# The copy of the first Q group of each query tile, moved from VectorE to ScalarE

## The reference

```python
q, k, v = (einsum('bsm,hmd->bhsd', x, kernel[i]) for i in (0, 1, 2))
attn = softmax(einsum('bhsd,bhtd->bhst', q, k) / (64*64*16))
x = layernorm(x + einsum('bsf,fm->bsm', (attn @ v)_as_b_s_f, WO[0]))
x_prev = x shifted by one token
r = sigmoid((mu_r*x + (1-mu_r)*x_prev) @ W_r.T)
kk = (mu_k*x + (1-mu_k)*x_prev) @ W_k.T
x = layernorm(x + r * (square(relu(kk)) @ W_v.T))
```

## Time and profile before

| | |
|---|---|
| median of 3 runs | 2562.26 us (2561.67 to 2564.42) |
| profiled execution | 2560.9 us, span 2559.4 us on the slowest core |
| spans of the 8 cores | 2553.3 to 2559.4 us |
| PE busy | 2079.9 us, 81% |
| ACT busy | 1245.6 us, 49% |
| DVE busy | 833.8 us, 33% |
| granted TensorE clock, mean of the slowest core | 0.893 |

### The profile page before, as it was taken

The page is one execution under the profiler, slowest core; times in us unless marked ns, Lnnn a source line. Parts: engine busy times, 40 slices in busy tenths (PEclk is TensorE's granted clock), DMA queues, the critical chain, the costliest instruction groups (busy, mean ns, idle before and its releaser), DMA issues.

```text
span 2559.4 us, 29992 instructions; the slowest of 8 cores (2553.3 to 2559.4 us)
## 1 busy us (share of the span) xinstructions
PE 2079.9 (81%) x10062; PEld 709.3 (28%) x10176; DVE 833.8 (33%) x1369; ACT 1245.6 (49%) x1441; POOL 20.2 (1%) x27
## 2 busy tenths in 40 slices
PE   0998888798888978896898888878978897889835
PEld 0442222232222222232342222222222232223212
DVE  0330014233341525053550140432434052504356
ACT  0017855756375637653006556475627663665520
POOL 0000000000000000000000000000000000000000
PEclk9998888898989989898899999988888898889867
DMA  9359600013100420033221130101310041002201
GB/s 182 46 81 203 164 12 23 1 67 97 52 1 34 116 66 1 34 99 83 33 50 33 40 109 34 34 1 66 83 66 1 34 116 66 1 1 72 99 28 65
DMA packets 83056, 153.04 MB, mean 60 GB/s; under 512 B 1952, under 2 KB 16352, under 8 KB 82912
## 3 DMA queue, kind: packets, MB, share of 16 engines
q1 hardware_dynamic: 51184, 102.87, 12.4%
q0 software_dynamic: 23024, 31.47, 8.6%
q10 hardware_dynamic: 8704, 16.78, 1.9%
HBM read 151.12 MB, written 31.46 MB: 71 GB/s over the span
## 4 chain that ended last, share of the span: by engine, by line
PE 58%; ACT 20%; DVE 11%; issue 8%; another core or an unknown queue 2%; ACTq 1%; DMA 1%; DVEq 0%; POOLq 0%
PE psg L99 29%; ACT pb L109 13%; PE pspv L99 11%; PE psden L99 11%; ACT lta L109 5%; PE psa L99 4%; PE psb L99 3%; DVE xka L118 2%; DVE rg L118 2%; DVE stv L118 2%; ACT rcr L109 1%; DVE recb L118 1%; DVE y L118 1%; DVE xra L118 1%
## 5 line engine op out<-in xcount | busy, mean ns | idle before, releaser
L109 ACT ACTIVATE pb<-psa 128x1024 bf16<-128x1024 f32 x512 | 522.8, 1021 | 381.7 <-PE psa L99 380.4
L109 ACT ACTIVATE pb<-psb 128x1024 bf16<-128x1024 f32 x512 | 523.8, 1023 | 363.8 <-PE psden L99 191.4
L99 PE MATMUL pspv<-pb,vtb 128*64 128x512 bf16 x2048 | 429.4, 427 | 19.9 <-DVE aba L118 19.8
L99 PE MATMUL psden<-pb,cstb 128*32 128x512 bf16 x2048 | 412.6, 411 | 0.0
L99 PE MATMUL psg<-xra,ws 128*128 128x512 bf16 x1264 | 342.1, 421 | 9.3 <-issue 8.9
L99 PE MATMUL psa<-qtb,ktb 64*128 64x512 bf16 x1024 | 214.6, 406 | 142.9 <-ACT pb L109 82.9
L118 DVE TENSOR_TENSOR aba<-pspv,rsb 128x512 bf16<-128x512 f32 x64 | 44.3, 692 | 766.7 <-ACT rsb L109 765.7
L99 PE MATMUL psb<-qtb,ktb 64*128 64x512 bf16 x1024 | 208.4, 401 | 62.2 <-ACT pb L109 62.2
L99 PEld LDWEIGHTS pspv<-pb,vtb 128*64 128x64 bf16 x2048 | 111.0, 109 | 282.6 <-issue 282.6
L99 PEld LDWEIGHTS psg<-xra,ws 128*128 128x128 bf16 x1320 | 128.1, 105 | 198.9 <-issue 93.3
L99 PE MATMUL psg<-aba,ws 128*128 128x512 bf16 x373 | 96.5, 413 | 87.4 <-DMA aba<-xT 78.1
(11 more groups left out here) (113 smaller groups left out, 1680.6 us busy)
## 6 DMA issues: line engine op xcount, KB each, us to landing
ws<-wsc SPq DMA_DIRECT2D x34, 2048.0 KB, 9.6
ws<-wts POOLq DMA_DIRECT2D x8, 2048.0 KB, 22.4
y<-xT SPq DMA_DIRECT2D x8, 2048.0 KB, 13.1
outT<-outb ACTq DMA_DIRECT2D x32, 512.0 KB, 4.6
wsc<-ws SPq DMA_DIRECT2D x7, 2048.0 KB, 16.1
xra<-xT POOLq DMA_DIRECT2D x6, 1024.0 KB, 12.7
aba<-xT POOLq DMA_DIRECT2D x4, 1024.0 KB, 13.4
rg<-xT POOLq DMA_DIRECT2D x4, 1024.0 KB, 9.7
```

What stands on the lines that cost most here:

```text
L99: i = e.matmul(_o, _l, _r, start=_st, stop=_sp, tile_position=_tp, skip_group_check=True)
L109: i = e.activation(_o, _i, _f, scale=_s, bias=_b)
```

## The change

The copy of Q group 0 of each tile is made by ACT (`AF.Copy`) instead of DVE. Its bank is freed by `c_ar` instead of `c_vg`, and the scores of head pair 0 wait for `c_ar`. Since the counter now differs, `qev` holds the counter beside the value. Groups 1 to 7 stay as they were. Eight copies of an execution are moved, one for each query tile.

```diff
                 def qevac(b):
-                    wait("v", c_g)
-                    nv = vop("tensor_copy",
-                             (QTB[:, oc * QT:(oc + 1) * QT], b.ap[:, :]),
-                             inc=c_vg)
-                    b.free = (c_vg, nv)
-                qev[oc] = 0
+                    if oc == 0:
+                        wait("a", c_g)
+                        nv = act(QTB[:, 0:QT], b.ap[:, :], AF.Copy, inc=c_ar)
+                        b.free = (c_ar, nv)
+                        qev[oc] = (c_ar, nv)
+                    else:
+                        wait("v", c_g)
+                        nv = vop("tensor_copy",
+                                 (QTB[:, oc * QT:(oc + 1) * QT], b.ap[:, :]),
+                                 inc=c_vg)
+                        b.free = (c_vg, nv)
+                        qev[oc] = (c_vg, nv)
                 proj_group(WS[2], oc, xbch, qevac)
-                qev[oc] = c_vg.n
...
                     if kt == 0 and qev.get(hp):
-                        wait("t", c_vg, qev[hp])
+                        wait("t", qev[hp][0], qev[hp][1])
```

## The result

The changed kernel takes 2522.85 us (median of 9 runs); the kernel before has 2564.85 us over its 10 runs by now. The ratio is 0.9843, with a 95% interval of 0.9820 to 0.9867: about 40 us or 1.6% faster. The profiled execution took 2517.97 us, against 2560.9 us before: 42.9 us less. Some executions of every kernel are slower on one die, at a lower granted clock; ratios and comparisons leave them out.

What follows compares the result with a forecast made beforehand. PE was taken to pace the kernel, idling for DVE's late copy. Six tiles gain 43.8 us, first tiles lose 0.9: 42.9 off 2560.9 gives 2518.0, median 2519 us, range 2505 to 2531.

Steps and rivals of the forecast that it cites:

- What the wait is, and that it goes: First scores, six non-first tiles: PE idles 9.57 us for a copy behind DVE's chain; on ACT, scores start 8.73 us earlier.
- That DVE is the next to be late, at the fourth Q group: Fourth Q group needs the second's bank, freed by DVE behind its chain: PE waits 1.87 us.
- One of the signs of being wrong that I named: At a tile's start: the idle that precedes the previous tile's adds grows; no size given.
- The cap of 9.0 us: Start of the fourth Q group: DVE's bank limits the gain to 397.20 - 388.20 = 9.0 us a tile.
- That the wait brings the low clock, one group's worth a tile: After the new wait, one Q group at the lower clock in each of six tiles, costing 1.69 us each.
- The likeliest case: One Q group at low clock after the new wait in each of six tiles: 2519 us, chance 0.50.
- the clock stays up: Rival: no clock drop after the new wait before the fourth Q group; gain 53.1 us, 2509 us, chance 0.22.
- Net a tile: Six non-first tiles: 9.0 us gained less 1.7 us for low clock, 7.3 us a tile.
- The first tiles: First tile of each sequence: 1.1 us lost to the table load, about 0.2 us gained; together -0.9 us.
- second load: ACT in the first tile: if copy and exp needed two table loads, 1.3 us more lost; none expected.
- The transfers: Weight load in 379 to 388, now beside PE's work: counted as nothing, at most 0.3 us a tile.
- Sum: Whole kernel: 43.8 - 0.9 = 42.9 us off 2560.9 gives 2518.0 us; median 2519 us.

Runs made afterwards that it cites:

- e1_q01_act: The changed kernel with the second Q group's copy on ACT as well: 2512.14 us, ratio 0.9796 to the kernel before.
- e11_dbl_chain: The changed kernel with DVE's max/square chain of 16 operations done twice in each tile: 2590.79 us in the profiled execution.
- e4_not_first: The changed kernel with the first Q group's copy back on DVE in the first tile of each sequence: 2507.94 us, set against the changed kernel's profiled execution.
- e6_not_first: The same kernel as e4_not_first, run again and timed: 2508.54 us, ratio 0.9768 to the kernel before.
- e7_dve_place: The changed kernel plus a one-column DVE memset in each first tile, in place of the copy taken from DVE: single times 2512.37 and 2508.37 us.
- e5_after: The changed kernel itself, run again: 2522.63 us, ratio 0.9812 to the kernel before.
- e8_warm_table: The changed kernel plus a one-column exp on ACT at the very start, to load the table early: 2522.88 us, ratio 0.9815 to the kernel before.
- e2_order_dve: The kernel before, all copies on DVE, the 16-operation chain emitted behind the first Q group's copy in tiles 2 to 4 of each sequence: 2525.54 us, ratio 0.9853.
- e3_split_dve: The kernel before, all copies on DVE, a quarter of the chain behind each copy of Q groups 2 to 5: 2501.34 us, ratio 0.9754.
- e9: The same kernel as e3_split_dve, run a second time: ratio 0.9768 to the kernel before.

## Why the prediction was right, point by point

- *What the wait is, and that it goes.* Right. The forecast was scores 8.73 us earlier, capped at 9.0; the idle of PE fell by 9.57 - 0.94 = 8.6 us, and the gap by 9.07 (with the slow first scores gone). ACT's copy took 0.597 us, and the hand-overs were within 0.1 us of those of the earlier trace rows (0.94 us in all against 0.84).
- *That DVE is the next to be late, at the fourth Q group.* Right in place, shown from both sides by e1_q01_act and e11_dbl_chain. The size, 1.87 us in the forecast and 1.93 to 1.96 measured, agrees because two errors cancel: DVE's pause adds 0.35 us, and without it (e4_not_first) the wait is 1.58 to 1.61, 0.27 us under the forecast, since PE comes 0.18 us later and the bank is free 0.09 us earlier than I took. One of the signs of being wrong that I named did come, in one tile: in the second tile of the first sequence the idle before the last adds grew from 2.17 to 2.53 us, and that is the same pause. It was in the trace of the kernel before, unread: one of the six waits there is 9.92 us where the earlier trace rows has 9.57.

```profile
938.15 0.61 PE L99 MATMUL psa<-qtb,ktb 64*128 64x512 bf16 x2 [9.92 <-DVE qtb L118]
```

- *The cap of 9.0 us.* Read 0.2 us too high. The fourth group of the earlier trace rows, at 397.20, has x7; its weight loads show that it starts at 396.97, so the cap was 8.8 us, and by it 53 us in six tiles instead of 54:

```profile
396.97 1.41 PEld L99 LDWEIGHTS psg<-xra,ws 128*128 128x128 bf16 x8 [0.23 <-issue]
```

- *That the wait brings the low clock, one group's worth a tile.* Right for this kernel, 45 of 48 times, but for a finer reason than I gave. I set 1.87 us beside the 1.82 us of the earlier trace rows. At this place the clock never fell in the 144 tiles of e4, e6 and e7, with waits of 1.58 to 1.61 us; with waits of 1.93 to 1.98 us, in the changed kernel, e5 and e8, it fell in 126 of 136 tiles. The length alone doesn't decide: it also fell in all eight tiles of e8_warm_table whose wait was only 1.69 us, and it stayed up in six tiles of e2_order_dve with 2.41 us. The likeliest case was the measured one because the pause came on top; without the pause the rival "the clock stays up" would have been the true one, at 2508 us, near the 2509 that it was given.

  The Trainium skill ("TensorE: Matmul & The Clock Gate", "HAM oscillation — how this bites in real kernels") prices a throttled stretch at half of its length; 3.3 us of low clock in steps 0 to 16 give 1.6 us by it, and the runs agree: 30.37 against the 28.48 of e6_not_first is 1.9 us, of which 0.35 is the longer wait.
- *Net a tile.* 7.3 us in the forecast, 9.07 - 1.89 = 7.2 measured.
- *The first tiles.* A term too small: 1.1 us forecast for the table load, about 2.2 measured on six cores, since the 2.12 us of idle also brought the low clock on the second group, and 0.6 on the two where it didn't. No second load came, as in the row of the page.
- *The transfers.* Right: the second and third group take 1.90 us each beside the weight load (DMA share 1.00 in 384 to 388).
- *Sum.* Forecast for the profiled execution 2518.0 us, measured 2517.97; for the median 2519, measured 2522.85. The first closeness is partly luck: the mean span of the 8 cores fell from 2556.6 to 2510.8, by 45.8 us, while the slowest core lies 5.5 us above the mean now and lay 2.8 above it before. Steps 16 to 127 became 0.6 us a tile shorter, which no term of the sum has. The medians fell by 40 to 42 us.

What stays open: what DVE does in its pause. Where it pauses is shown, not why. Open too is what beside the length of a wait decides whether the clock falls, and why the low clock lasts longer in steps 16 to 60 when the tile's start is faster.

## What to carry to other kernels

When a copy is late, look first at what stands before it in its engine's list: moving that behind or between the copies (e3_split_dve) won some 64 us, where the other engine for the one late copy won 42. When a wait is removed, follow the banks and buffers of the same engine's next operations, for they say where the next wait ends. A wait of a length after which the clock here sometimes fell and sometimes didn't makes a kernel sensitive to changes that have nothing to do with it: compare such waits in the traces before putting 10 us down to the edit. And before reading a wait off a row, count its matmuls: if the first one's record is missing, the wait reads too long, and the weight loads show the true start.

## What the runs showed that I had not expected

- Two DVE operations fewer in the first tiles, off the path, cost 10 to 14 us: a pause of 0.35 us that stands at fixed places of DVE's instruction list, 59 more than a multiple of 128, made a wait of PE 1.93 to 1.96 us instead of 1.58 to 1.61, and with it came the low clock (e5_after against e7_dve_place: first 16 steps 30.5 against 28.48 us).
- Speed at a tile's start is in part given back as low clock later in the tile: without the wait (e1, e3, e9) steps 16 to 60 have 21.0 to 22.5 us at the low clock, against 18.3 and 16.4 in the two traces of the changed kernel, and take 0.4 to 1.6 us longer. That the one causes the other isn't shown.
